# Digit copy in the sort stage of a graph network kernel: ScalarE with a bias column in place of VectorE

## The reference

```python
feat = relu(einsum('nd,ohdk->ohnk', x, W) + b)            # layer 0: self and neighbour parts, 4 heads of 32
att_s, att_n = leaky(feat[0] . a_self), leaky(feat[1] . a_neigh)
edge_w = (att_s[:, src] + att_n[:, dst]) * edge_weight
agg = segment_sum(edge_w * feat[1][:, dst, :], src)       # summed by src
x = layernorm(x + norm_per_head(feat[0], agg) * scale + offset)
messages = relu(concat(x[src], x[dst]) @ W_msg + b_msg)   # layer 1
agg = segment_sum(messages, dst)                          # summed by dst
h = relu(concat(x, agg) @ W_upd + b_upd)
out = layernorm(x + layernorm(h) * gamma + beta)
```

## Time and profile before

| | |
|---|---|
| median of 3 runs | 4115.1 us |
| the profiled execution | 4111.97 us, span 4110.2 us |
| PE busy | 3755.8 us, 91% |
| DVE busy | 3431.8 us, 83% |
| ACT busy | 2781.4 us, 68% |
| POOL busy | 2763.5 us, 67% |

### The profile page before, as it was taken

One profiled execution on the slowest core, in us unless ns is written; L12 is line 12 of the kernel. 1 busy time (PEld: TensorE's weight loads), 2 busy tenths in 40 slices (PEclk: granted clock), 3 DMA queues, 4 the chain that ended last, 5 costly groups with the idle time before them and its releaser, 6 DMA issues.

```text
span 4110.2 us, 86275 instructions
## 1 busy us (share of the span) xinstructions
PE 3755.8 (91%) x26503; PEld 3151.8 (77%) x26503; DVE 3431.8 (83%) x7664; ACT 2781.4 (68%) x7163; POOL 2763.5 (67%) x2817
## 2 busy tenths in 40 slices
PE   4999999989999999999689989898898989988886
PEld 3999999978888888888477767677677777776764
DVE  7999999979999999999577777777777777777776
ACT  3777877767777777777466666666666666666664
POOL 2887899944454455544477777777777777777774
PEclk9999999999999999999899999999999999999998
DMA  5676544466777777776345555555555555545544
GB/s 127 223 237 222 194 178 171 177 196 189 201 205 211 203 209 206 203 211 195 119 148 159 158 153 156 157 152 154 154 159 153 150 160 154 159 152 160 156 151 91
DMA packets 345349, 710.35 MB, mean 173 GB/s; under 512 B 58425, under 2 KB 201606, under 8 KB 344866
## 3 DMA queue, kind: packets, MB, share of 16 engines
q0 software_dynamic: 115680, 361.28, 32.1%
q1 hardware_dynamic: 229218, 343.52, 24.7%
HBM read 510.45 MB, written 195.74 MB: 172 GB/s over the span
## 4 chain that ended last, share of the span: by engine, by line
PE 41%; POOL 29%; issue 17%; DVE 8%; DMA 4%; SPq 1%; ACT 1%; DVEq 0%; ACTq 0%; POOLq 0%
POOL arena L801 29%; PE ps L1308 21%; PE ps L1330 3%; DMA arena<-d_p,tabs 3%; PE ps L1290 3%; PE ps L1342 3%; PE ps L1156 2%; PE ps L1146 2%; DVE big L1610 1%; DVE tabs L1610 1%; PE ps L1363 1%; PE ps L1365 1%; PE ps L1141 1%; PE ps L1220 1%; PE ps L1163 1%
## 5 line engine op out<-in xcount | busy, mean ns | idle before, releaser
L801 POOL DMA_INDIRECT arena<-d_p,tabs x1628 | 1566.9, 962 | 540.0 <-issue 487.1
L1330 PE MATMUL ps<-arena 128*128 128x256 f32 x3256 | 862.5, 401 | 84.1 <-DVE big L1899 79.5
L1342 PE MATMUL ps<-big,scr 128*128 x3256 | 812.3, 389 | 135.9 <-DVE arena L1909 125.0
L787 POOL DMA_INDIRECT arena<-d_m,scr x392 | 531.1, 1355 | 578.8 <-DVE arena L1752 251.2
L1112 ACT ACTIVATE arena<-arena 128x1024 f32<-128x1024 f32 x407 | 430.1, 1057 | 712.0 <-DVE arena L1909 711.5
L1899 DVE SCALAR_TENSOR_TENSOR big<-big,tabs,ps 128x256 f32 x1628 | 773.8, 475 | 105.6 <-DVE big L1899 94.0
L1909 DVE TENSOR_TENSOR arena<-arena,ps 128x512 f32<-128x512 f32 x814 | 524.9, 683 | 395.5 <-DMA arena<-d_p,tabs 331.6
L1342 PEld LDWEIGHTS ps<-big,scr 128*128 128x128 f32 x3256 | 620.9, 194 | 259.1 <-issue 174.0
L1330 PEld LDWEIGHTS ps<-arena 128*128 128x128 f32 x3256 | 607.9, 196 | 272.1 <-DVE big L1899 128.8
L1308 PE MATMUL ps<-arena,scr 128*128 128x256 f32 x2620 | 609.7, 383 | 2.6 <-DVE arena L1752 2.6
L997 ACT ACTIVATE arena<-arena 128x128 f32<-128x128 f32 x1310 | 410.9, 389 | 193.4 <-PE ps L1308 182.7
(11 more groups left out here) (284 smaller groups left out, 5993.7 us busy)
## 6 DMA issues: line engine op xcount, KB each, us to landing
d_m<-arena SPq DMA_DIRECT2D x108, 603.0 KB
arena<-d_loc SPq DMA_DIRECT2D x136, 384.0 KB, 4.2
d_m<-arena SPq DMA_DIRECT2D x108, 402.0 KB
arena<-d_p,tabs POOLq DMA_INDIRECT x1628
arena<-in_xT_dram SPq DMA_DIRECT2D x96, 256.0 KB, 4.8
d_xp<-arena SPq DMA_DIRECT2D x49, 256.0 KB, 3.3
arena<-d_xp SPq DMA_DIRECT2D x49, 256.0 KB, 4.1
d_x<-arena SPq DMA_DIRECT2D x49, 256.0 KB, 4.4
```

Of the source, the lines that this page charges most:

```text
L787: e.indirect_dma_start(out=GB[g % 4].rearrange("p a b -> p (a b)"), out_offset=None, in_=runs_m, in_offset=bass.IndirectOffsetOnAxis(ap=TI ...
L801: e.indirect_dma_start(out=G1[j % 8][:, k, :], out_offset=None, in_=d_p, in_offset=bass.IndirectOffsetOnAxis(ap=tabS[:, j, k:k + 1], axis= ...
L1330: m = e.matmul(turn(H, AB)[:, k * 256:k * 256 + 256], OH1[(j - 2) % 4][:, 2 * h + k, :], G1[(j - 2) % 8][:, 2 * h + k, :], start=True, sto ...
L1342: m = e.matmul(turn(H, QB)[:, k * 256:k * 256 + 256], OT1[j % 2][:, 2 * h + k, :], big[:, ts[2 * h + k] + 1, :], start=True, stop=True)
```

## The change

A column `C_M1` that holds -12582912 is added to the constants. The digit copy is removed from VectorE's `sort` and made by ScalarE in step j = q + 5 as an activation (Identity) with that column as bias, behind the copy of the tile totals (L943) and ahead of `evict(x, 1)`. It waits for `U2` of the same step (`s_v`), and for the readers of the digits of the batch before (`s_c`, `s_or`). VectorE's `U2` gets a wait for the digit copy of the batch before (`s_q`), since that reads `U2`.

```diff
+C_M1 = C_RK + 1
+CW = C_M1 + 1
...
                     e.activation(TOTS[b % 2][0:NT, :], PS[b % 2][0:NT, 128:256], ACT.Copy).then_inc(S("s_ts"), 1)
+                if 0 <= j - 5 < NB:
+                    waitn(e, "s_v", j - 4)
+                    waitn(e, "s_c", j - 5)
+                    waitn(e, "s_or", j - 5)
+                    e.activation(QD[L], U2[L].unsqueeze(2).to_broadcast([LANES, COLS, 2]), ACT.Identity, bias=c[L, C_M1:C_M1 + 1]).then_inc(S("s_q"), 1)
                 if 0 <= x < NB:
                     evict(x, 1)
...
-            u = U2[L].unsqueeze(2).to_broadcast(b2)
...
                     waitn(e, "s_rk", q + 1)
+                    waitn(e, "s_q", q)
                     e.tensor_scalar(U2[L], RKP[L], 1.0 / PC, M1, ALU.mult, ALU.add).then_inc(S("s_v"), 1)
...
-                if 0 <= q < NB:
-                    waitn(e, "s_v", q + 1)
-                    waitn(e, "s_or", q)
-                    e.tensor_scalar(QD[L], u, -M1, None, ALU.add).then_inc(S("s_q"), 1)
...
+    c[:, C_M1] = -M1
```

More of the change, by code:

```diff
@@ L50 @@
 C_RK = C_LIM + NB
-CW = C_RK + 1
+C_M1 = C_RK + 1
+CW = C_M1 + 1
 M16, M1, M64 = 201326592.0, 12582912.0, 805306368.0
```

## The result

| | changed kernel | kernel before |
|---|---|---|
| median | 4087.04 us (4085.99 to 4089.81, 4 runs) | 4114.33 us (4112.77 to 4116.34, 4 runs) |
| the profiled execution | 4089.81 us, span 4088.1 us | 4111.97 us, span 4110.2 us |

The ratio is 0.9934, 95% interval 0.9917 to 0.9952: faster, by 27.3 us between the medians and by 22.2 us between the two profiled executions. The predicted time was 4094.7 us, in a range of 4087 to 4112 us.

The account below looks back on a forecast made before the run. VectorE, partly held up by GpSimd, was taken to bound the late sort at 6.578 us a step. Savings of 20.0 + 1.0 - 0.6 = 20.4 us from 4111.97 gave 4091.6, plus 3.1 to the median: 4094.7 us, range 4087 to 4112.

Parts of the forecast that it names:

- What bounds the sort: Early sort: TensorE and VectorE both full at 7.69 us a step; late sort: VectorE sets 6.578 us, 0.72 lost to GpSimd.
- The copy's slot, 0.20 us sure: In VectorE's late step, removing the digit copy surely saves its undisturbed slot of 0.20 us.
- The copy on ScalarE, 0.28 us: In ScalarE's step the added copy takes 0.28 us, making 5.5 us busy; not a bound, even at 0.34.
- The hold puts F 2.5 us behind, once: Late sort: ScalarE's wait for `U2` moves F to about 2.5 us behind VectorE's reduction, losing TensorE's lead only once.
- The pace, 6.2 us: Late step with F at 2.5 us: mean of two measured steps, 6.415, less 0.20 is 6.215, taken as 6.2 us.
- the first rival, TensorE's floor: Late sort: VectorE drops below TensorE's 6.11 us a step; gain 25.2 us, so 4089.9 us; chance 0.2.
- Seam and run-out: Where the two regimes meet, 1.0 us gained (0 to 1.5); at the sort's end, 0.6 us lost (0 to 2.2).
- The sum: Whole sort: 20.0 us from 53 late steps, plus 1.0, less 0.6, together 20.4 us less.
- The hold is only moved: Late sort: GpSimd's hold on VectorE passes to another instruction, step 6.37 us; gain 11.4 us, so 4103.7 us; chance 0.25.
- GpSimd is the true pace: Late sort: GpSimd's queue can't go below about 6.5 us a step; gain 4 us or less, 4112 us; chance 0.12.
- Both instructions hit: Late sort: L767 and L769 each hold a long VectorE instruction; step 6.86 us, 15 us more, 4130 us; chance 0.08.
- The signs: Expected in the profile after: late steps of 6.2 us, ScalarE waiting for `U2` each step, last reduction near 810 us.

Follow-up runs that it names:

- e7: Kernel before with TensorE's expansion in two passes of three, 15 of 103 matmuls a step less; ratio 1.0002, late step 6.590 us.
- e5: Kernel before with GpSimd's subtraction and comparison cut to one column of fifteen from the third batch on; ratio 0.9933.
- e1: Kernel before, VectorE keeping its copy, plus the same activation and wait on ScalarE into an unread spare tile; 4103.8 us against 4110.6, ratio 0.9982.
- e8: Changed kernel with TensorE's expansion in two passes of three; ratio 0.9923, late step 6.221 us.
- e9: Kernel before with the digit copy made by nobody after a first one and TensorE's expansion in two passes of three; ratio 0.9950, late step 6.431 us.
- e2: Kernel before with the digit copy made by nobody after a first one, so no activation or hold on ScalarE; 4083.6 us, ratio 0.9937.
- e6: Changed kernel with GpSimd's subtraction and comparison cut to one column of fifteen from the third batch on; ratio 0.9929.
- e11: The changed kernel run once more, unaltered, on another chip; ratio 0.9946, late step 6.135 us.
- e3: Changed kernel with ScalarE's digit copy moved to the head of its step, ahead of the first expansion eviction; 4091.3 us, ratio 0.9950.
- e4: Changed kernel with ScalarE's digit copy moved later in its step, behind the third expansion eviction; 4106.3 us, ratio 0.9986.

## Why the prediction was right, and where not

The measured 4087.04 us lies 0.04 us above the lower end of the range, and two of the four runs lie below it. That it is inside is luck; the forecast proper, 4089 to 4098 us, was missed. The direction and the kind of gain were right, the size of the pace and of the part ahead of it were not.

**What bounds the sort.** Right. The early regime stayed at 7.68 us a step; the late one was VectorE's (e7), stretched by GpSimd's pair (e5). VectorE's own work was put too high, though: 5.86 us less the copy's 0.20 is 5.66, and the changed kernel has steps of 5.59. The 0.72 us of stretch left out the product with the payload (1.03 us for 0.96). And "L767 waits for F, so it moves with TensorE's phase" does not hold in the kernel before: L767 starts at 607.15 without a wait, when GpSimd is through with its copy. It holds in e1 and e8.

**The copy's slot, 0.20 us sure.** Right: e1 less e8, with and without the slot and with F at nearly the same place, is 6.420 - 6.221 = 0.20 us.

**The copy on ScalarE, 0.28 us.** It takes 0.33 us (606.46), near the 0.34 that was allowed for, and as there it changes nothing.

**The hold puts F 2.5 us behind, once.** Right as a mechanism: e1 (2.6 us) and e8 (2.4 us) against e9 (0.32). But in the changed kernel it is nearly idle. TensorE comes out of the node work 2.5 us behind VectorE by itself. From there the kernel before fell back to 0.34 since VectorE was the slower engine; with the copy gone VectorE is fast enough at that phase never to be caught (e2). I had seen this starting point and made the hold responsible for keeping it.

**The pace, 6.2 us.** This is the mis-sized term. It was worked out for the phase with F at 2.5 us and is right there: 6.221 us in e8, and 6.420 in e1 against the mean of 6.415 that I read. But in the changed kernel F isn't held there: from step 55 on it stands by turns 2.5 and 3.1 us behind, later up to 4.8, and pairs fall on L1601, L1606 and L1637 in every second step only. Against 5.59 that is 0.53 us a step in the mean, where the state of e8 loses 0.63. That is the first rival, TensorE's floor, whose 6.11 us e5 and e6 measure as 6.118. I gave it a chance of 0.2 because two steps at 2.5 us had lost more, as if the phase could not move on.

**Seam and run-out.** I had 20.0 + 1.0 - 0.6. Measured on F: 20.3 us over the 53 steps, 1.7 ahead of them, 0.2 behind, together 22.2. The run-out was over-feared: 0.2 us gained for 0.6 lost. The part ahead was 0.7 us larger than said, and it didn't come from the seam alone. Against the kernel before F is 1.4 us late from step 9 to step 36, 1.0 us early at step 37, 1.1 at step 52 and 1.7 at step 54. So the seam gave 0.6 us, and 2.4 us came from one step in the middle of the node work, which no term of the sum had. At the start of step 36 VectorE has two instructions on the edge lists, 2.07 and 1.03 us long (L1569 and L1572). TensorE then waits for ScalarE, which waits for VectorE. The kernel before:

```profile
311.97 2.07 DVE L1569 TENSOR_TENSOR big<-big,arena 128x1664 f32<-128x1664 int32 x1
```

```profile
324.32 0.53 PEld L1156 LDWEIGHTS ps<-arena,scr 128*128 128x128 bf16 x9 [2.27 <-ACT arena L916]
...
328.60 0.15 PEld L1216 LDWEIGHTS ps<-big 116*128 116x128 f16 x1
```

```profile
326.00:330.00 4.00, 4.00 (x37) 3.38 (x36) 3.93 (x10) 1.94 (x5) 0.00 (x0) 0.63 0.37 154
```

and the changed one:

```profile
324.58 0.53 PEld L1162 LDWEIGHTS ps<-arena,scr 128*128 128x128 bf16 x9 [1.12 <-ACT arena L917]
...
327.60 0.10 PEld L1222 LDWEIGHTS ps<-big 116*128 116x128 f16 x1
```

From F to F this step is 11.35 us in the kernel before and 8.94 in the changed one. Without the copy VectorE had got 1.0 us further ahead of TensorE (F 6.2 us behind the reduction instead of 5.2), so the wait is 1.15 us shorter. Behind the longer wait the granted clock was at its lower level (1.2 GHz) for a part of the next stretch, 0.63 in the mean of 326 to 330 us; in the changed kernel it stayed at 1.00. The rest of the 2.4 us goes with that. The prediction had this lead at 0.4 us, ended by the wait at L1621, and said that nobody needs it. It was 1.0 us, with hardly a wait at L1621, and it was needed at this one long piece of work.

**The sum.** 22.2 us measured against 20.4 between profiled executions: 1.8 us off. The other 5 us to the median are an offset: the profiled execution of the changed kernel was the slowest of its four, that of the kernel before below all its timed runs, and the offset of 3.1 us that I carried over was a matter of one execution. On e11's chip the medians differ by 23.2 us (0.9932 to 0.9960), so the gain is some 22 to 27 us.

**The rivals.** "The hold is only moved" (of GpSimd's lock on VectorE) is real without ScalarE's hold and with a short TensorE: e9 gains 6.590 - 6.431 = 0.16 us a step, and L1618 has taken over what the copy and L1610 lost. The Trainium skill's rule of the exclusive lock ("SBUF — State Buffer", section "Who interferes with whom") says that the waiting engine stalls until the other's instruction is through, and the trace agrees on how long the wait lasts: in e9 L1618 starts at 605.52, GpSimd's L769 runs from 605.62 to 606.20, and L1618, 0.19 us long by itself, ends at 606.24. Which of the two was first the rows don't tell: L1618 is listed as starting 0.10 us ahead of L769, but L1613 ahead of it ends at 605.60 only. "GpSimd is the true pace" is out: it keeps up with steps of 6.12 us at 298.02 of 322 us busy, and in e3 it even waits 27.6 us for F in 39 such steps, so much of its busy time was being held. "Both instructions hit" came true in kind in e4 and e9 (0.52 and 0.17 us) but at 6.431 - 5.66 = 0.77 us of loss on the prediction's count, short of the 0.92 from which it would have been slower; e4 shows that it could be near.

**The signs.** L1616 back near 1150 ns and TensorE's 0.45 us wait gone: seen. ScalarE's wait for `U2` in each late step, late steps of 6.2 us each and L1624 or L1633 longer: not seen, for the reason above. VectorE's short waits at L1621 early: one, of 0.3 us, from 143 to 440 us. The last reduction is at 804.6 us, not near 810. A step that isn't even over the regime was named as a sign against me, and it was one: 5.59 and 6.65 us by turns.

## What to carry to other kernels

Where two engines exclude each other, an instruction's cost depends on where in the step the other one stands. So read the phase between the two (here GpSimd's pair behind the reduction) as well as the busy time, and ask what places it: a wait for a third engine, as for F in e1 and e8, or the two queues alone. VectorE and GpSimd meet here at more than semaphores, other than the section on the cores says. A step estimate taken in one phase holds only while no engine is slower than the one that it was made for; then take the floor of that engine instead.

The place of a moved instruction isn't free because nobody waits for it: 1.45 us later in ScalarE's queue lost 15.7 of 22.2 us here, while ahead of its input, with a wait in front, the late steps were as good as with the change. Look as well for single steps that hold more work than the others; a steady-state sum passes over them.

## What the runs showed of the hardware

- Less work on one engine made another slower: with 15 of TensorE's matmuls a step fewer, VectorE's late step grew from 6.132 to 6.431 us (e2, e9) and from 6.118 to 6.221 us (after, e8). VectorE's instructions were the same; what changed is on which of them GpSimd's pair fell (3.38 and 3.8 us behind the reduction, instead of 5.34 and 0.10 by turns).
- A 32-column VectorE instruction of 0.20 us takes 0.72 us when GpSimd's 0.58 us subtraction starts 0.1 us after it (e4, e9): it gets done only when that is through. A short instruction can lose as much as a long one (0.52 us, against 0.54 for the 128x1920 comparison in the kernel before).
- GpSimd's comparison takes 0.82 us in e1, 1.41 in the changed kernel and 1.78 in e4, at the same shape and at different places beside VectorE's work, so its busy time says little of its load.
- TensorE's granted clock fell to its lower level in the middle of the sort of the kernel before (0.63 as the mean of 326 to 330 us) after TensorE had waited 2.27 us; in the changed kernel, where it had waited 1.12 us at the same place, the clock stayed at 1.00.
- The same program (kernel before) took 4111 to 4114, 4468 and 4482 us on different chips. The late steps of the sort agree to 0.3%. From 1500 us on the stages are slower: TensorE was busy 860.0 of the 1000 us from 1500 us on in e7, and 921.3 in the kernel before, with the same code there.
